# A factorised recommendation tower on one core: how the first group of pair products is made, when embedding rows are gathered, and one pass less over the rectified maps

## The reference, cut to what matters

```python
e = stack([tbl_f[ids[:, f]] for f in range(32)], axis=1)      # (512, 32, 32)
x0 = prev = e
for W in (filter_0, filter_1):                                  # (1024, 128), (4096, 128)
    z = einsum('bhd,bmd->bhmd', x0, prev).reshape(b, h * m, d)
    cur = relu(einsum('bpd,pn->bnd', z, W[0]))
    prev = cur; outs.append(cur)
z = sum(concatenate(outs, axis=1), axis=-1)                     # (512, 256)
h = concatenate([z, dense_ctx], axis=1)
h = maximum(h @ W_top1 + b_top1, 0); h = maximum(h @ W_top2 + b_top2, 0)
y = h @ W_top3
```

## Time and profile before

| what | us |
|---|---|
| median of 3 runs (lowest, highest) | 870.16 (868.09, 870.87) |
| the profiled execution | 867.69 |
| its span, first to last instruction | 865.9 |
| TensorE busy | 842.2 (97%) |
| ScalarE, GpSimd, VectorE busy | 798.3, 754.7, 747.8 |

### The profile page before, as it was taken

How to read it: one execution, slowest core, us unless ns; L and a number is a source line. 1 busy time by engine, 2 the same in 40 slices (tenths; PEclk the granted TensorE clock), 3 DMA queues, 4 the chain that set the end, 5 groups by cost and what they waited for, 6 DMA issues and landing times.

```text
span 865.9 us, 16597 instructions
## 1 busy us (share of the span) xinstructions
PE 842.2 (97%) x3584; PEld 667.0 (77%) x3584; DVE 747.8 (86%) x800; ACT 798.3 (92%) x2781; POOL 754.7 (87%) x544
## 2 busy tenths in 40 slices
PE   2899999999999999999999999999999999999998
PEld 1688777778877777887777887777788777788776
DVE  4588888998888898888889888889888888988894
ACT  2699999999999999999999999999999999999994
POOL 5599999999999999999999999999999899997661
PEclk9999999999999999999999999999999999999999
DMA  5452222212222211222221222222122222122000
GB/s 163 140 148 83 77 81 83 60 34 78 80 77 81 80 47 44 82 76 80 82 79 28 64 82 76 80 81 54 36 81 79 77 81 69 35 69 73 2 1 1
DMA packets 42924, 61.11 MB, mean 71 GB/s; under 512 B 6259, under 2 KB 17139, under 8 KB 42902
## 3 DMA queue, kind: packets, MB, share of 16 engines
q1 hardware_dynamic: 38806, 58.75, 22.2%
q0 software_dynamic: 4096, 2.11, 1.6%
HBM read 56.64 MB, written 4.20 MB: 70 GB/s over the span
## 4 chain that ended last, share of the span: by engine, by line
PE 94%; DVE 2%; DMA 2%; issue 1%; SPq 0%; POOL 0%; ACT 0%; DVEq 0%; POOLq 0%
PE ps_y L685 27%; PE ps_y L686 27%; PE ps_y L691 27%; PE ps_c L664 6%; PE ps_c L674 2%; PE ps_c L672 2%; PE ps_c L673 2%; DVE csum L581 1%; PE ps_c L670 1%; DMA second<-et_scratch 1%; DVE prod L568 1%; DMA gat<-table,rows_now 1%; PE ps_h L696 0%; POOL gat L306 0%; DMA et_scratch<-gat 0%
## 5 line engine op out<-in xcount | busy, mean ns | idle before, releaser
L433 ACT ACTIVATE prod<-ps_y,es 128x128 f32<-128x128 f32 x2560 | 720.8, 456 | 26.8 <-PE ps_y L691 21.0
L581 DVE TENSOR_REDUCE csum<-prod 128x64 f32<-128x1536 f32 x256 | 446.4, 1744 | 0.1
L685 PE MATMUL ps_y<-w_hi,c_hi 128*128 128x512 f32 x1024 | 428.5, 419 | 0.9 <-ACT c_hi L394 0.5
L691 PE MATMUL ps_y<-w_hi,c_lo 128*128 128x512 f32 x1024 | 400.2, 391 | 0.0
L686 PE MATMUL ps_y<-w_lo,c_hi 128*128 128x512 f32 x1024 | 400.1, 391 | 0.0
L568 DVE TENSOR_TENSOR prod<-ps_y,es 128x512 f32<-128x512 f32 x384 | 259.0, 681 | 89.9 <-PE ps_y L691 89.8
L344 POOL TENSOR_TENSOR prod<-prod 128x1024 f32<-128x1024 f32 x128 | 309.1, 2415 | 27.4 <-ACT prod L433 22.0
L685 PEld LDWEIGHTS ps_y<-w_hi,c_hi 128*128 128x128 f32 x1024 | 192.5, 188 | 56.3 <-issue 10.5
L686 PEld LDWEIGHTS ps_y<-w_lo,c_hi 128*128 128x128 f32 x1024 | 192.5, 188 | 53.7 <-issue 14.9
L691 PEld LDWEIGHTS ps_y<-w_hi,c_lo 128*128 128x128 f32 x1024 | 192.2, 188 | 42.1
L335 POOL TENSOR_TENSOR z<-first,second 128x512 f32<-128x512 f32 x155 | 198.7, 1304 | 9.7 <-DMA second<-et_scratch 9.7
(11 more groups left out here) (96 smaller groups left out, 287.2 us busy)
## 6 DMA issues: line engine op xcount, KB each, us to landing
second<-et_scratch SPq DMA_DIRECT2D x160, 256.0 KB, 4.3
first<-et_scratch SPq DMA_DIRECT2D x32, 256.0 KB, 3.3
et_scratch<-gat SPq DMA_DIRECT2D x64, 64.0 KB
prod<-w SPq DMA_DIRECT2D x4, 512.0 KB, 7.8
gat<-table,rows_now POOLq DMA_INDIRECT x128, 2.4
wt_sb<-wt SPq DMA_DIRECT2D x2, 512.0 KB
prod<-w0a SPq DMA_DIRECT2D x1, 320.0 KB, 3.3
prod<-w0b SPq DMA_DIRECT2D x1, 320.0 KB, 3.3
```

Source lines behind the costliest of these rows:

```text
L433: last = nc.scalar.activation(prod[:, buffer_of(g, u), h // 2, :, h % 2], ps_y[:, bank_of(g, u, k), j * N:(j + 1) * N], ACT.Copy, scale=es ...
L581: nc.vector.tensor_reduce(csum[:, g.r, maps, u], prod[:, buffer_of(g, u), FOLD // 2:F // 2, maps, :].rearrange("p a n t -> p n a t"), AX.X ...
L685: nc.tensor.matmul(out, hi, w_hi, start=True, stop=False)
L691: nc.tensor.matmul(out, lo, w_hi, start=False, stop=True).then_inc(y_ready, 1)
```

## The change

There are six edits.

1. Group 0's pairs no longer go through DRAM. `row_picks` makes 0/1 matrices, which are loaded into `picks_sb` (cleared by a GpSimd memset first). TensorE multiplies the gathered rows by them: six sets (`first` and five shifts) of four f32 matmuls, each 128 by 128 columns into a part of `ps_y`. ScalarE copies the `first` set out, VectorE multiplies it by the five others. In group 0, four of the five parts of `z` then go in full f32 (four calls in place of two, without splitting), the last as before.
2. The gathers of groups 0 to 2 read their row numbers straight from `rows`, and VectorE computes the row numbers of these 12 tiles first. Only a quarter of filter 1 is loaded ahead of them; the other three quarters are issued when group 0's rows are in.
3. Later groups' row numbers are put into `rows_now` by a SyncE transfer (`stage`), one group ahead, in place of the GpSimd copy. Group 3's is issued after the pair loads of group 2.
4. The warm-up has 10 matmuls in place of 22, and waits only for the filter and constants.
5. The remainders of filter 1 (`rest_w1`) are spread over the start and the first tile. The first two banks of group 0 have their `c_hi` matmuls ahead of their `c_lo` ones.
6. `rectify_whole` and `c` are gone. `c_hi` and `c_lo` lie side by side in `c_both`, and `sum_h0` sums both, 1024 columns in place of 512; the wait on `c_ready` becomes one on `c_lo_ready`.

```diff
-WARM_UP = 22
+WARM_UP = 10
+FIRST_ROWS = SLOTS * TG
+PICKS = {"first": 0, 0: 1, 1: 2, 2: 3, 3: 4, 4: 5}
+PICK_ORDER = (4, 0, 1, 2, 3)
...
+            def filters(n):
+                fields = slice(n * F // W1_LOADS, (n + 1) * F // W1_LOADS)
+                sp.dma_start(w1_raw[:, fields, :], w1[:, fields, :]).then_inc(w1_in[n], 16)
+
+            filters(0)
             sp.dma_start(w0a_sb, w0a).then_inc(w0_in, 16)
             sp.dma_start(w0b_sb, w0b).then_inc(w0_in, 16)
             sp.dma_start(copy_sb[:, :], copy_of).then_inc(w0_in, 16)
+            sp.wait_ge(picks_zeroed, 1)
+            for q in range(BT):
+                sp.dma_start(picks_sb[q * F:(q + 1) * F, q, :, :], picks).then_inc(picks_in, 16)
             sp.dma_start(ones_b[:, :], ones_of_b).then_inc(ones_in, 16)
+            sp.wait_ge(gathered[0], 16 * TG)
+            for n in range(1, W1_LOADS):
+                filters(n)
+
+            def stage(g):
+                sp.dma_start(rows_now[:, g.r, :], rows[:, bass.ds(g.times(TG), TG)]).then_inc(rows_staged, 16)
...
-            pairs(Group(0, 0))
             for g in range(1, SLOTS):
                 pairs(Group(0, g))
+            sp.wait_ge(rows_step, 10)
+            sp.wait_ge(rows_past, 1)
+            stage(Group(0, SLOTS))
...
-                nc.gpsimd.tensor_copy(rows_now[:, g.r, :], rows[:, bass.ds(g.times(TG), TG)]).then_inc(rows_staged, 1)
-                pool.wait_ge(rows_staged, g.times(1, 1))
+                    pool.wait_ge(rows_staged, g.times(16, 16 * (1 - SLOTS)))
...
-            def rectify_whole(g):
-                act.wait_ge(c_lo_ready, g.times(1, 1))
-                act.wait_ge(h0_done, g.times(1))
-                nc.scalar.activation(c[:, :], ps_c[:, :], ACT.Relu).then_inc(c_ready, 1)
...
+            def multiply_picked(k, place):
+                dve.wait_ge(picked, place)
+                nc.vector.tensor_tensor(z[:, k, :], first[:, :], ps_y[:, PICKS[k], :], ALU.mult).then_inc(z_ready, 1)
...
-                dve.wait_ge(c_ready, g.times(1, 1))
+                dve.wait_ge(c_lo_ready, g.times(1, 1))
                 nc.vector.tensor_reduce(
-                    h0[:, bass.ds(g.times(GB), GB)], c[:, :].rearrange("p (o b d) -> p b o d", b=GB, d=DT),
+                    h0[:, bass.ds(g.times(GB), GB)],
+                    c_both[:, g.r, :].bitcast(F32).rearrange("p (o b d) -> p b o d", b=GB, d=DT),
                     AX.XY, ALU.add).then_inc(h0_done, 1)
...
-            pe.wait_ge(es_ready, 1)
             for n in range(WARM_UP):
                 nc.tensor.matmul(ps_y[:, 0, :], w0_hi[:, 0, :], w0_hi[:, 0:BANK // N, :].rearrange("p k n -> p (k n)"),
                                  start=True, stop=True)
+            pe.wait_ge(picks_in, 16 * BT)
+            pe.wait_ge(gathered[0], 16 * TG)
+            for load in ("first",) + PICK_ORDER:
+                table_of, shift = {"first": (1, 0), LASTK: (1, P // 2)}.get(load) or (0, 16 * load)
+                for q in range(BT):
+                    last = nc.tensor.matmul(ps_y[:, PICKS[load], q * P:(q + 1) * P], picks_sb[:, q, table_of, shift:shift + P],
+                                            gat[:, 0, :], start=True, stop=True)
+                last.then_inc(picked, 1)
             for k in range(KP):
-                layer0(Group(0, 0), k)
-            pe.wait_ge(w_ready, 3)
+                layer0(Group(0, 0), k, 0)
```

200 lines of the change are left out of this document (119 added, 81 removed).

## The result

The changed kernel took 876.34 us (median of 6 runs, 874.73 to 876.68) beside 869.85 for the kernel before (6 runs); the ratio is 1.0083, interval 1.007 to 1.0096. It is slower by 6.5 us. The forecast was 867.3, the range 864.5 to 870.8, with 0.1 for slower. The profiled execution took 876.64, its span is 874.8, and so 8.9 us longer than that of before.

A forecast was written before the change was run, and what follows sets the result against it. TensorE was taken to bound the kernel until the last group, VectorE its end. Start -5.8, row-number stall +2.4 and longer sum +0.54 give -2.86; taken from the median 870.16 that is 867.3 us, range 864.5 to 870.8.

The forecast's parts named there:

- Filter 0 ready at 9.95: Start: filter 1's 512 KB ahead of filter 0's loads delays filter 0 by 1.5 us, to 9.95.
- Ten slow warm-up matmuls, 4.3 us; picks 0.25 a call: Start: warm-up at the slow spacing of 0.43 us ends at 14.2; 24 picking calls take 6.0 us plus 0.4.
- (c): Start, rival: loading and streaming of the picks do not overlap, 0.43 us a call, 871.6 us in all; chance 0.10.
- (d): Start, rival: a Trainium skill rule puts weight load plus 128-column matmul at 81 ns; 865.2 us in all; chance 0.05.
- VectorE's product keeps pace: Start: VectorE's 0.68 us product of a set keeps up with one set a microsecond, ending before TensorE needs it.
- The start is worth what layer 1 gains: Start: layer 1 begins at 24.9 in place of 30.69, counted in full as -5.8 us.
- The transfer lands 3.3 us after its issue, +2.4: Group 3's row numbers by SyncE: the gather comes 2.4 us late, all of it a stall in group 1.
- (b): Group 3's row numbers, rival: the transfer waits for everything ahead, 4.2 us, 869.1 us in all; chance 0.14.
- The lower bound: Group 3's row numbers: the transfer lands 1.7 us after issue in an empty queue, the gather 0.7 us later.
- The longer sum, +0.54 at the end, since VectorE has no wait there: Last group: `sum_h0` over 1024 columns takes 1.21 us, adding 0.54 us at the end; hidden in the middle.
- its last sum ending about 27.4 + 0.5 us after the wait: Last group, expected sign: VectorE's last sum ends that long after the wait ahead of the group's first banks.
- The remainders of filter 1 in the first tile lie under waits: Group 0's first tile: VectorE's 2 x 0.65 and ScalarE's 2 x 0.6 us fall where both waited for TensorE's first banks.

The follow-up runs named there:

- g1: The changed kernel run again with nothing altered: 872.34 us, ratio 1.0039 to the kernel before.
- f2: Changed kernel with load-free warm-up, filter 0 loaded first, group 3's row numbers early, dense_x's remainder earlier, group 2's gathers held until group 0's products end: 863.18 us.
- f4: Changed kernel with group 3's row-number transfer before the pair loads of groups 1 and 2, and dense_x's remainder one reduction earlier: 865.30 us.
- e1: Changed kernel with group 3's row-number transfer issued before the pair loads of groups 1 and 2: 870.88 us, ratio 1.0017.
- e5: Kernel before with only the one pass over the maps (no second ScalarE pass, VectorE sums 1024 columns): 869.32 us, ratio 1.0001.
- e3: Changed kernel with the two passes restored (ScalarE writes `c` again, VectorE sums 512 columns): 871.37 us, ratio 1.0026.
- e9: Changed kernel with one more VectorE instruction (a 0.06 us memset) at the start of the program: 871.50 us, ratio 1.0033.
- e2: Changed kernel with VectorE's remainder of dense_x one reduction earlier in the last group: 872.65 us, ratio 1.0039.
- e6: Kernel before with VectorE's remainder of dense_x two instructions later in the last group, inside GpSimd's fold: 870.79 us, ratio 1.0016.
- g2: f4 with the last four gathers, of group 2, held until group 0's products are done: 876.15 us, ratio 1.0081.
- e4: Kernel before with VectorE's remainder of dense_x one instruction later in the last group: 869.45 us, ratio 0.9998.

## Why the prediction was wrong, step by step

*Filter 0 ready at 9.95.* It was ready at 11.9; the load put ahead of it costs 2.8 to 3.6 us, not 1.5. Mis-sized, and it carried through: the warm-up ends at 16.44, not at 14.2.

*Ten slow warm-up matmuls, 4.3 us; picks 0.25 a call.* 4.4 and 0.235. Right. The rivals (c) and (d) are out: 0.235 is not 0.43, and each of a call's two pairs of records takes 0.12 us, not 0.081.

*VectorE's product keeps pace.* In three sets of six. With it (g1) the start gains 4.7 of the 5.8 forecast: the picks begin 1.8 us later than forecast because of filter 0, and cheaper calls give part of that back. Without it (first result) the start gains 3.4.

*The start is worth what layer 1 gains.* Only down to about 25 us. f2 starts layer 1 at 20.49 and f4 at 25.03, but group 2's pair stands at 80.13 and 80.71: GpSimd's products of group 1 begin at 27.5 and 27.4, each time when their loads land. The pair loads of group 1 are the next bound, and the forecast did not look for it.

*The transfer lands 3.3 us after its issue, +2.4.* It landed after 5.4, with everything ahead of it, and cost 5.0 (e1), 4.85 (f4 against g1), twice the forecast. The mechanism was right, the size was that of rival (b) and some 0.7 us more. The lower bound was not one for an empty queue either: the `bounds` load that gave the 1.7 us was issued 0.49 us behind the 64 KB of ids. By the Trainium skill, "DMA: Bandwidth & Descriptors", section "Queues, rings and completion order", a small transfer waits for the bytes ahead of it in the ring; the 5.4 us for 2 KB, against 1.7 for the row transfers of the whole run, agree, and I should have given that bound more weight than the middle one.

*The longer sum, +0.54 at the end, since VectorE has no wait there.* This is the step that failed. The sum itself costs 0.53 (e5), but the stretch grew by 4.31. A chain without waits is not free to shift: its instructions stand against those of another engine. In the kernel before, dense_x's remainder began 1.28 us ahead of the fold. 0.53 us later from the sum, 0.40 us earlier for the fold (ScalarE's freed pass, which I had costed at nothing), and 0.37 us from the code's place are 1.30 us, and so the remainder began inside the fold. e3 takes away the first two and e9 the third, and e2 moves the remainder; all three cure it, and e6 makes a collision without any of the change. That it came to lie 0.01 us behind the fold's start and not ahead of it was chance, but the prediction did not look at the distance at all. The Trainium skill, "SBUF — State Buffer", section "Who interferes with whom", says that a VectorE instruction with two SBUF inputs and a GpSimd instruction that reads SBUF contend for a shared port, which it calls an exclusive lock, and that the order of issue decides who blocks. e6 (1.92 us for VectorE, GpSimd first) and e9 (2.62 for GpSimd, VectorE first) agree in both orders. g2 does not: six of the seven GpSimd instructions that VectorE waited through began after it. No rival of mine was of this kind. The sign "its last sum ending about 27.4 + 0.5 us after the wait" does not come out of the earlier trace rows either: from 817.93 to 852.27 is 34.3 us, and in the changed kernel, from 820.19 to 858.47, it was 38.3.

*The remainders of filter 1 in the first tile lie under waits.* In the changed kernel one of them took 1.69 us in place of 0.68, beside a product of GpSimd, and TensorE did not wait for it. In g2 the same instruction took 9.92, and TensorE waited 8.1. The cover was there, but not the safety that the forecast read into it.

*The end.* The clock was 0.54 to 0.78 between 857 and 867 us in the changed kernel, 1.00 before. I first gave the change the 2.7 us. But 15.0 to 15.2 and 16.3 us occur with and without a collision, in kernels close to the one before too (e4 and e5 with 15.1, e6 with 16.3), and 13.63 in the one profile of the kernel before only. g1 has 15.17 with the same code as 16.33. So some 1.5 us of the span's difference are most likely the luck of the first profile and 1.2 that of the second, not the change's; the medians, which average over it, show 6.5 and not 8.9.

What the change does, then: in the first result start -3.4, stall +5.3, last group +4.3, in sum +6.2 beside the medians' 6.5. In a set at pace (g1) start -4.7, stall +4.65, last group +4.25, in sum +4.2; g1's medians say +3.2, and its profiled execution, 873.4, was 1.1 above its median.
